# Attention kernel on one Trainium2 core: the remainders of q, k and v move from GpSimd to VectorE, and ScalarE writes the rounded probabilities of four units with a second exponential

## What is computed

```python
h = _layernorm(x) * (1 + ca) + sa
q, k, v = (tanh(h @ W + bias) for W, bias in ((Wq, bq), (Wk, bk), (Wv, bv)))   # 16 heads of 64
alpha = softmax(where(causal, q @ k.T / sqrt(64), min))
x = x + ga * tanh((alpha @ v) @ Wo + bo)
```

## Time and profile before

| | kernel before |
|---|---|
| timed runs, median (lowest to highest) | 2969.16 us (2967.93 to 2970.8) |
| the profiled execution, its own time | 2966.9 us |
| its span in the trace | 2965.1 us |
| TensorE matmul busy | 2543.7 us (86%) |
| VectorE busy | 2031.3 us (69%) |
| ScalarE busy | 1586.9 us (54%) |
| GpSimd busy | 860.4 us (29%) |
| mean granted TensorE clock | 0.951 of full speed |

### The profile page before, as it was taken

The page is one execution under the profiler, slowest core; times in us unless marked ns, Lnnn a source line. Parts: engine busy times, 40 slices in busy tenths (PEclk is TensorE's granted clock), DMA queues, the critical chain, the costliest instruction groups (busy, mean ns, idle before and its releaser), DMA issues. The chain is left out here.

```text
span 2965.1 us, 66220 instructions
## 1 busy us (share of the span) xinstructions
PE 2543.7 (86%) x21520; PEld 1926.9 (65%) x21520; DVE 2031.3 (69%) x4373; ACT 1586.9 (54%) x3034; POOL 860.4 (29%) x732
## 2 busy tenths in 40 slices
PE   5689988989998999189999996799799999994996
PEld 3466656666666666167777775688577777773885
DVE  5588668858885886657777775566577777773656
ACT  2566557646664665346656654333356656652332
POOL 0233223313332332234334333111243343341111
PEclk7899999999999999689999998899899999997998
DMA  4400020010002000400000000100100000000003
GB/s 146 154 11 12 10 69 16 11 50 30 16 11 69 11 16 6 151 6 0 7 0 7 2 5 5 47 0 0 34 0 7 0 7 0 7 0 7 0 0 113
DMA packets 74547, 77.26 MB, mean 26 GB/s; under 512 B 4225, under 2 KB 67321, under 8 KB 72953
## 3 DMA queue, kind: packets, MB, share of 16 engines
q1 hardware_dynamic: 74488, 76.46, 7.8%
HBM read 55.48 MB, written 16.78 MB: 24 GB/s over the span
## 5 line engine op out<-in xcount | busy, mean ns | idle before, releaser
L501 ACT ACTIVATE at_p<-at_ps_s,at_shift 128x1024 f32<-128x1024 f32 (+3 forms) x384 | 343.0, 901 | 112.2 <-DVE at_p_lo L435 50.7
L435 DVE TENSOR_TENSOR at_p_lo<-at_p,at_p_hi 128x1024 f16<-128x1024 f32 (+3 forms) x384 | 391.4, 1019 | 12.1
L431 DVE CAST at_p_hi<-at_p 128x1024 f16<-128x1024 f32 (+3 forms) x384 | 283.1, 737 | 140.7 <-PE at_ps_o L569 99.6
L1017 ACT ACTIVATE ly_probs<-ly_masked,ly_small,ly_rq 128x256 f32<-128x256 f32 x512 | 302.3, 592 | 63.9 <-DVE ly_small L1200 63.3
L74 PE MATMUL ly_ps<-ly_w_hi,ly_operands 128*128 128x512 f32 (+1 forms) x792 | 294.1, 371 | 15.3 <-DVE ly_operands L1150 8.7
L567 PE MATMUL at_ps_o<-at_v,at_p_hi 128*128 128x65 f16 x2304 | 249.1, 194 | 36.0 <-DVE at_p_lo L435 36.0
L567 PEld LDWEIGHTS at_ps_o<-at_v,at_p_hi 128*128 128x128 f16 x2304 | 209.3, 96 | 100.2 <-DVE at_p_lo L435 56.6
L75 PE MATMUL ly_ps<-ly_w_lo,ly_operands 128*128 128x512 f32 (+1 forms) x792 | 274.0, 346 | 0.0
L76 PE MATMUL ly_ps<-ly_w_hi,ly_operands 128*128 128x512 f32 (+1 forms) x792 | 273.1, 345 | 0.0
L1403 PEld LDWEIGHTS ly_ps<-ly_values,ly_probs_T 128*128 128x128 f32 x2048 | 258.3, 191 | 15.4 <-issue 0.4
L1403 PE MATMUL ly_ps<-ly_values,ly_probs_T 128*128 x2048 | 259.6, 270 | 0.0
(11 more groups left out here) (209 smaller groups left out, 6362.4 us busy)
## 6 DMA issues: line engine op xcount, KB each, us to landing
at_hT<-hT_hi SPq DMA_DIRECT2D x5, 1024.0 KB, 5.4
at_hT<-hT_lo SPq DMA_DIRECT2D x5, 1024.0 KB, 8.1
at_w_raw<-in_Wv SPq DMA_DIRECT2D x34, 128.0 KB, 2.2
at_w_raw<-in_Wq SPq DMA_DIRECT2D x34, 128.0 KB, 2.3
at_w_raw<-in_Wk SPq DMA_DIRECT2D x34, 128.0 KB, 2.4
n_x<-in_states SPq DMA_DIRECT2D x4, 1024.0 KB, 11.7
hT_hi<-n_hi SPq DMA_DIRECT2D x8, 512.0 KB, 3.0
hT_lo<-n_lo SPq DMA_DIRECT2D x8, 512.0 KB, 3.1
```

Source lines behind the costliest of these rows:

```text
L431: dve.tensor_copy(p_hi[u % 2][:, :, off:], probs[u % 2][:, :, off:]).then_inc(p_hi_done, 1)
L435: dve.tensor_tensor(p_lo[u % 2][:, :, off:], probs[u % 2][:, :, off:], p_hi[u % 2][:, :, off:], ALU.subtract).then_inc(p_lo_done, 1)
L501: act.activation(probs[u % 2][:, :, off:], ps_s[u % 2][:, :, off:], ACT.Exp, bias=shift[:], scale=SCORE_SCALE).then_inc(exp_done, 1)
L1017: step = act.activation(pr[:, j % 2, h, :], sm[:, j % 2, h, :], ACT.Exp, bias=small[:, j % 2, 1, h:h + 1], scale=rq[:, par, 2 * j + h:2 * ...
```

## The change

- GpSimd keeps its memsets and loses all six subtractions per head pair. VectorE does them: for projection i at unit u (PROJ_AT) right behind its remainder of unit u, and the six of the very first pair ahead of the loop.
- For units 0, 4, 5 and 8 (ACT_HI; each 128x1024) ScalarE writes the f32 exponential and then, once the value products of unit u - 2 are done, the same exponential of the same scores again, to the f16 tile p_hi. Only the second counts exp_done up. VectorE no longer casts these units; for the other eight (DVE_HI) it does, as before.

```diff
+ACT_HI = (0, 4, 5, 8)
+DVE_HI = [u for u in range(NU) if u not in ACT_HI]
+NHI = len(DVE_HI)
...
             @block.gpsimd
             def _(pool):
-                pool.sem_inc(pj_lo, CREDIT)
                 pool.memset(shift[:], SCORE_SHIFT).then_inc(const_done, 1)
...
-                    hold(pool, tick, (pj_hi, at(base + i + 1)))
-                    pool.tensor_tensor(lo[:, cols], stage[:, i % 2, :], hi[:, cols], ALU.subtract).then_inc(pj_lo, 1)
-
-                for i in range(NPJ):
-                    split_projection(0, i, 0)
-                with pool.Fori(0, B) as b, pool.Fori(0, HP // 2) as j:
-                    for par in range(2):
-                        it = b * HP + j * 2 + par
-                        for i in range(NPJ):
-                            split_projection(NPJ * (it + 1), i, 1 - par)
...
+                    dve.wait_ge(pj_hi, at(base + i + 1))
+                    dve.tensor_tensor(lo[:, cols], stage[:, i % 2, :], hi[:, cols], ALU.subtract).then_inc(pj_lo, 1)
...
                 split_weights(0)
+                for i in range(NPJ):
+                    split_projection(0, i, 0)
                 dve.wait_ge(pj_mm, at(NPJ))
...
-                                dve.tensor_copy(p_hi[u % 2][:, :, off:], probs[u % 2][:, :, off:]).then_inc(p_hi_done, 1)
+                                if u in DVE_HI:
+                                    dve.tensor_copy(p_hi[u % 2][:, :, off:], probs[u % 2][:, :, off:]).then_inc(p_hi_done, 1)
                                 if u == CT - 1 + LAG:
                                     normalise(it * NC, it * NU + CT)
-                                dve.wait_ge(p_hi_done, at(it * NU + u + 1))
+                                if u in DVE_HI:
+                                    dve.wait_ge(p_hi_done, at(it * NHI + DVE_HI.index(u) + 1))
                                 dve.tensor_tensor(p_lo[u % 2][:, :, off:], probs[u % 2][:, :, off:],
                                                   p_hi[u % 2][:, :, off:], ALU.subtract).then_inc(p_lo_done, 1)
+                                if u in PROJ_AT:
+                                    split_projection(NPJ * (it + 1), PROJ_AT[u], 1 - par)
...
-                                act.activation(probs[u % 2][:, :, off:], ps_s[u % 2][:, :, off:], ACT.Exp,
-                                               bias=shift[:], scale=SCORE_SCALE).then_inc(exp_done, 1)
+                                step = act.activation(probs[u % 2][:, :, off:], ps_s[u % 2][:, :, off:], ACT.Exp,
+                                                      bias=shift[:], scale=SCORE_SCALE)
+                                if u in ACT_HI:
+                                    act.wait_ge(pv_done, at(it * NU + u - 1))
+                                    step = act.activation(p_hi[u % 2][:, :, off:], ps_s[u % 2][:, :, off:], ACT.Exp,
+                                                          bias=shift[:], scale=SCORE_SCALE)
+                                step.then_inc(exp_done, 1)
```

More of the change, by code:

```diff
@@ L371, in _, with split_weights @@
                     pool.memset(v[i][:, :, :, DH:DH + 2], 1.0).then_inc(const_done, 1)
+            @block.vector
+            def _(dve):
+                for s in (p_hi_done, p_lo_done, pj_lo, wl_done, r_done, cx_done, vt_lo, ct_lo, yg_done, x1_done):
+                    dve.sem_inc(s, CREDIT)
+                def split_weights(n):
+                    dve.wait_ge(wh_done, at(n + 1))
+                    dve.tensor_tensor(w_lo[:], w_raw[:], f32(w_hi[:]), ALU.subtract).then_inc(wl_done, 1)
                 def split_projection(base, i, dst):
```

## The result

The changed kernel took 2975.68 us (median of 20 runs, 2972.29 to 2979.94) against 2967.50 us for the kernel before beside it (20 runs): ratio 1.0028, interval 1.0021 to 1.0035. That is 0.28% slower, 8.2 us (the interval is 6.2 to 10.4 us). The profiled execution took 2976.59 us with a span of 2974.2.

What follows compares the result with a forecast made beforehand. No engine bounds the whole period: TensorE the second half, waits on ScalarE and VectorE the first. 0.40 + 0.27 + 0.20 - 0.55 = +0.32 us per pair, +8.1 us with the differing pairs: 2977.3 us, range 2955 to 2990.

Steps and rivals of the forecast that it cites:

- Where the period's length is made: Per head pair: TensorE full in the second half; first half waits on ScalarE's rounded tanh and VectorE's copy into at_v.
- Term 1: First half, ScalarE: unit 0's second exponential delays the transposes of v by 0.76 us, less 0.36: +0.40 us per pair.
- the 0.36: First half: slack before unit 4's exponential, which VectorE's remainder of unit 2 released, not its scores; 0.36 us.
- Term 2: First half: unit 4's second exponential on ScalarE replaces VectorE's cast on the chain, 2.14 us for 1.87: +0.27 per pair.
- Term 3: Second exponentials of units 5 and 8: +0.27 each on their own chains, covered by 0.4 and 2 us: 0.
- Term 4: Six remainders on VectorE: five covered, the sixth delays unit 11's cast in the pair's tail: +0.20 us per pair.
- term 5: Pair's tail: unit 11's cast, no longer blocked by GpSimd, takes 0.29 us instead of 0.84: -0.55 per pair.
- The pairs that differ: The very first pair, forecast at -0.7 us, and the three opening a later batch, -0.08 each, -0.2 together.
- Rival A: First half: unit 0's second exponential is covered, so a pair goes -0.44 us: faster, 2956 us; chance 0.2.
- Its long form: VectorE's relief counts in full, 2.2 us per pair: about 2899 us; chance 0.03.
- Rival B: Pair's tail: the sixth remainder isn't in the way, +0.12 us per pair: within the noise, 2971.7 us; chance 0.24.
- Rival C: Units 5 and 8 exposed before their value products, +0.54 us more per pair: slower yet, 2992 us; chance 0.12.

Runs made afterwards that it cites:

- e2: The changed kernel with the second exponential for unit 0 alone; 2964.64 us, ratio 0.9991 to the kernel before.
- e1: The changed kernel without any second exponential, VectorE casting all twelve units; 2948.26 us, ratio 0.9933 to the kernel before.
- e9: The kernel before with VectorE's copy into at_v moved ahead of unit 4's cast, nothing else; 2944.70 us, ratio 0.9923.
- e5: The kernel before with the four second exponentials, remainders of q, k and v still on GpSimd; 2983.43 us, ratio 1.0058.
- e3: The changed kernel with the second exponential for unit 4 alone; 2952.87 us, ratio 0.9949 to the kernel before.
- e4: The changed kernel with second exponentials for units 5 and 8 alone; 2944.32 us, ratio 0.9920 to the kernel before.
- e12: e11 with no second exponential at all; 2909.51 us, ratio 0.9805 to the kernel before.
- e8: The changed kernel with second exponentials for units 5 and 8 alone, copy into at_v early, sixth remainder late; 2931.48 us, ratio 0.9879.
- e6: The changed kernel with the sixth remainder moved behind the weights' remainder at the pair's end; 2975.86 us, ratio 1.0034.
- e10: e6 with the remainder of the first chunk's context also moved behind the second chunk's normalisation; 2965.41 us, ratio 0.9992.
- e11: e8 with the first chunk's normalisation ahead of the wait for unit 5's exponentials and the context's remainder late; 2910.22 us, ratio 0.9802.

## Why the prediction was right

The time was forecast at 2977.3 us, 0.27% over the kernel before; it is 2975.68 and 0.28%. The mechanism holds step by step, as below; that forecast and measured difference agree to 0.1 us (8.1 and 8.2) is luck, because the terms were not known that well. By its own steps:

- **Where the period's length is made.** TensorE bounds the second half, ScalarE's chain and the copy bound the first: shown. The second half kept its length in the changed kernel (13.81 us against 13.82), e2 against e1 shows ScalarE's chain, and e9 shows that the copy was a bound.
- **Term 1, +0.40.** The transposes of v moved by 0.76 us behind the pair's first scores, the number worked out, but not all of it is the exponential's. The pair's own first exponential stands 2.54 us behind these scores now (415.40 to 417.94) and stood 2.50 behind before; from it to the last rounded tanh ScalarE takes 5.12 us (423.06) where it took 4.41 (415.90 to 420.31). That is 0.71, e5 has 0.72 for the transposes, and e2 against e1 gives 0.69 per pair: the slack was 0.29 us, where the prediction had 0.24. Of the delay the prediction let 0.36 vanish, because VectorE and not the scores had released unit 4's exponential. The exponential moved from 10.05 to 10.44 us behind the first scores, +0.39. Two traces bear the 0.36 out: from the last rounded tanh to this exponential there were 3.14 us before (420.31 to 423.45), and in e1, without GpSimd's subtractions and without a second exponential, 2.77 (417.00 to 419.77); and e1's -0.68 less the -0.33 of the tail leaves -0.35 per pair.
- **Term 2, +0.27.** 0.26 by e3 against e1; in the profile the remainder of unit 4 starts 2.15 us behind its exponential (425.84 to 427.99), where 2.14 was forecast.
- **Term 3, 0.** Shown by e4, and again by e12. The cover of unit 5 is the thin one: in the changed kernel the normalised context is ready at 430.93 and its products start at 431.37, 0.44 us later (0.4 forecast). In e8, with the copy out of the way, the wait comes up. It comes up in e9 too, which has no second exponential, so it isn't unit 5's exponential alone that makes it.
- **Term 4, +0.20, and term 5, -0.55.** The profile has 1.21 us where 1.22 was forecast and 1.02 was before, and a cast of 0.28; together e5 has them at -0.33. e6 and e10 show that the 0.20 is on the path, and that what stands behind it in VectorE's queue was equally near.
- **The sum** had +0.32 per pair; measured +0.29. The pairs that differ were forecast at -0.7 for the first (29.58 us between two roundings against 30.19, -0.6) and -0.2 for the three that open a batch (in all +0.4 for the distances that cross into them). Over the loop's 32 distances the trace has +7.55 us, against +8.1.
- **Rival A** (the second exponential of unit 0 is covered) fell: 0.69 us. Its long form, VectorE's relief counted in full, fell with e1. **Rival B** had the sixth remainder off the path; e10 speaks against it, though its number was only 4 us away. **Rival C** (units 5 and 8 exposed) fell with e4. The range of 2955 to 2990 was said to take in nearly all of C, but C's own point was 2992, outside of it; and B's 2971.7 keeps the +0.20 in the four pairs counted apart, without it the sum is about 1 us lower. Neither touches the forecast.
- The Trainium skill's rule on the shared ports (SBUF — State Buffer, Who interferes with whom), an exclusive lock held for the whole instruction, agrees with what the trace shows once GpSimd does none of the stage's subtractions: the 128x512 cast went from a mean of 859 ns to 424, the 128x256 one from 567 to 290, the 128x768 remainder from 1326 to 959, and e5 brought the casts back to 704 and 565. These are also the lengths alone that the prediction lacked when it set the slow 128x768 remainder and the 128x512 cast against another form's 0.69 us. But only some of this blocked time was on the chain: in e5 unit 2's cast and remainder are slow again (1.03 and 1.53 us), and unit 4's exponential still starts 0.94 us behind its scores, because ScalarE is later still.

What wasn't separated: the 0.36 us of VectorE's blocking in the first half follows from timelines, e1 and e5, not from a run that takes it away alone. And e10 is 2.4 us faster than the kernel before where its +0.02 per pair would make it about 0.6 us slower; of this difference of 3 us part lies in the first pair and between the batches (the loop's 32 distances sum to 0.8 us less than before), the rest outside the loop, where I have no cause for it.

## What to carry to other kernels

Before moving work to relieve a busy engine, find where in the period that engine is waited for: VectorE, the busiest after TensorE, was relieved by 54 us, and the kernel got slower, because two of four added instructions stood on ScalarE's chain. Four instructions of the same form cost 0.69, 0.26, 0 and 0 us per pair; the place decides, not the duration. And look first at the order in one engine's queue: an instruction that someone waits for, put ahead of one that waits itself, gave 0.8% by moving one copy, and the order gave 1.06 of the 1.74 us per pair of the best kernel.

## What the runs showed that I had not expected

- In e11 the first projection starts 0.39 us behind the remainder it needs, of which the profile puts 0.24 to issue; e10 has the same 0.39. The third projection of the kernel before, which waits for the copy, starts 0.06 behind it (427.14 to 427.20). In the code the first projection has two more waits behind that for the weights' remainder, the third has one wait only; whether that makes the difference is not shown, since no run varies the waits alone.
- In e6 VectorE's context remainder, whose input ScalarE had finished at 442.21, started at 442.36, 0.11 us behind the end of the instruction before it, while the reciprocal behind it, which doesn't wait, starts 0.08 before its predecessor's end. Removing 0.18 us ahead of it turned an unseen wait into a seen one.
